# One matmul per tile for the state and the outputs of a delta-rule scan, with GpSimd masking the state's keys and adding the state

## The chip, the cores and the metric

The kernel runs on one core of a Trainium2 chip. The metric is the device time of one execution in microseconds (us). Data is 32-bit float throughout. The core has five engines that run side by side and meet at semaphores: TensorE (PE; its weight loads are listed apart as PEld), VectorE (DVE), ScalarE (ACT), GpSimd (POOL) and SyncE (SP), which here issues the DMAs.

## The reference, cut to what matters

A gated delta-rule layer, then layer norm, then a linear layer with a low-rank addition, then layer norm. The input is 32 sequences of 512 tokens of width 256, 8 heads of 32. The costly part is the recurrence over the tokens: each (sequence, head) has a 32x32 state `S` that is read with the key, corrected, read with the query and decayed:

```
q, k, v = silu(x @ Wq), silu(x @ Wk), silu(x @ Wv);  k = k / |k|
beta = 2 * sigmoid(x @ Wbeta);  log_f = log_sigmoid(x @ Wf1 @ Wf2)
for every token, in two half steps (decay with the first, k v^T and the output with the second):
    bS = b_t . S
    S  = exp(g) * S + a_t (x) bS + k_t (x) v_t          # a_t = -beta * k (* exp(log_f)), b_t = k
    o  = q_t . S
y = rms_norm_per_head(o * sigmoid(x @ Wog1 @ Wog2)) * norm_w @ Wo
x = layernorm(x + y);  x = layernorm(x + x @ W^T + b + x @ lilora^T)
```

## The kernel before

The tokens are cut into blocks of 8 (`TB`), a block's 16 half steps (`ROWS`) are solved at once with the inverse of a 16x16 triangular matrix, and the blocks of a sequence follow each other through the state. Two sequences share a tile of 32 rows (`GB` = 2), four heads fill the 128 partitions (four quarters of 32), and a second half of four heads is a second tile, so a **chunk** is 8 tiles (`CT`) of 128x32. 512 tokens make a **group** of 8 chunks (`CH`); there are 32 groups (`G`).

PE works in **slots**, one a chunk, 8 a group (`slot`, L738). Slot n does three pieces of 32x32 work, each piece on the four quarters of the array side by side:

- `deltas` (L720): the inverse `t_now` times the right sides `x_now` of chunk n-1, into `p2_bank`;
- `updates` (L708), for chunk n-2: for each tile and head one matmul with the keys `w_now` stationary and `parts` moving (64 columns: the deltas of the one sequence, then of the other, the rest zero), which is the change of the state (`ds_bank`), and one with `delta` stationary and the masked query weights `aq_now` moving (16 columns), which is the part of the outputs that comes from within the block (`o_bank`);
- `right_sides` (L728): the state `s_now` with the keys and queries `uq_now` of chunk n, into `p1_bank` (24 columns).

Behind these three each slot has its own piece of dense work for other groups (`dense0` to `dense7`): slots 0 and 1 hold projections and four `scores` (L700, 48 columns), slot 2 the key projection and `turn_scores`, slot 3 the query projection and more, slot 4 `feed_forward`, slot 5 `sums`, slot 6 the output projection, slot 7 the transposes of the inverse. Every engine runs its own list in its written order, with semaphore waits in between; there is no scheduler.

Around a slot, once `updates` has finished (semaphore `p3_filled`): ACT copies `p2_bank` three times (`delta_part`, L851: masked for each of the two sequences into `parts`, plain into `delta`). DVE (`update`, L1073) subtracts the output parts (L1087, twice) and adds `ds_bank` to the state into `moved` (L1093); POOL multiplies `moved` with the decay back into `state` (`decay_part`, L473). When `right_sides` has finished, DVE subtracts the values (L1100) and turns the block (L1103) into `x_now`; ACT copies the queries' part (`query_part`, L863). SP stages the next operands (L382, L392, L394, L360, L361). Between these steps of the scan DVE does the rest of its list in a fixed order: in slot 3 the first eight steps of the 16x16 inverse (`solve`, L1141 and L1145), in slot 4 the other seven, in slot 5 the feed-forward's addition, the cumulative sums (L1227), L1233 and L1239, in slot 6 L1246, L1250 and L1257, in slot 7 L1266 and, as its last, the decayed keys and queries of the next group but one (L1277, L1282). The last of these releases SP's `stage_uq` (L350), whose DMA `scores` waits for in slot 0.

## Time and profile before

| | |
|---|---|
| time, median of 3 runs | 2630.47 us (2616.48 to 2632.16) |
| span of the profiled execution, first to last instruction | 2622.0 us |
| median less that span | 8.5 us |
| PE busy | 2288.4 us (87%) |
| DVE busy | 1601.7 us (61%) |
| ACT busy | 1618.0 us (62%) |
| POOL busy | 458.8 us (17%) |
| PE's share of the chain that ended last | 86%, and 10% issue |

The time of the profiled execution itself is not among the numbers shown; its span is, and the median stands 8.5 us above it. A share is a mean over the span: the stretches differ, and in a group of some 76 us DVE is far busier in slots 4 to 7 than in slots 0 to 3. "Issue" in the chain is time in which PE waits for nothing that the profile shows. The first window of rows 5 below holds slots 4 to 7 of a group, the second its slots 0 to 3. A matmul of 32-bit floats is two records on PE, so that the 32 matmuls of 64 columns in a slot are 64 records.

### The profile page before, as it was taken

How to read it: one execution, taken by the hardware profiler on the slowest of the kernel's cores; microseconds unless marked ns; L12 is line 12 of the kernel's file. 1: busy time of each engine (PE TensorE's matmuls, PEld its weight loads, DVE VectorE, ACT ScalarE, POOL GpSimd, SP SyncE). 2: the span in 40 equal slices, each digit the busy share in tenths (PEclk: the TensorE clock that was granted, in tenths of full speed). 3: DMA queues.
4: the chain of work that ended last, by engine and by line, in shares of the span. 5: the costliest groups of instructions: out<-in, count | busy, mean ns of one | idle time of the engine just before them, and what ended most of it. 6: DMA issues, size and time to landing. Idle time of an engine off the chain costs nothing.

```text
span 2622.0 us, 225147 instructions
## 1 busy us (share of the span) xinstructions
PE 2288.4 (87%) x102472; PEld 1721.9 (66%) x102472; DVE 1601.7 (61%) x3940; ACT 1618.0 (62%) x3048; POOL 458.8 (17%) x555
## 2 busy tenths in 40 slices
PE   6788898999988899998999998989999988999785
PEld 2556666666666666666676666666666666766573
DVE  2456366666556676656666665666666566666533
ACT  3556466666666666656666666666666666666543
POOL 1011111111111111111111111111111111111210
PEclk7879899999999999999999999999999999999987
DMA  3244455534555554455554455555445555534541
GB/s 95 74 110 121 110 148 148 141 104 127 145 141 151 137 141 111 132 138 146 144 137 118 124 145 146 148 141 142 113 129 143 145 148 148 136 103 132 140 125 41
DMA packets 692934, 338.90 MB, mean 129 GB/s; under 512 B 551794, under 2 KB 651728, under 8 KB 692816
## 3 DMA queue, kind: packets, MB, share of 16 engines
q1 hardware_dynamic: 692816, 337.67, 48.2%
q14 instruction: 86, 0.70, 0.1%
q8 instruction: 32, 0.52, 0.1%
HBM read 35.57 MB, written 16.78 MB: 20 GB/s over the span
## 4 chain that ended last, share of the span: by engine, by line
PE 86%; issue 10%; DVE 2%; ACT 1%; DMA 1%; SPq 0%; ACTq 0%; DVEq 0%
PE bank L570 14%; PE bank L733 13%; PE bank L712 11%; PE bank L704 8%; PE bank L724 7%; PE bank L716 5%; PE bank L593 5%; PE bank L683 5%; PE bank L622 5%; PE bank L643 3%; PE bank L577 3%; PE bank L694 2%; PE bank L602 2%; PE bank L587 2%; PE bank L584 2%
## 5 line engine op out<-in xcount | busy, mean ns | idle before, releaser
L473 POOL TENSOR_TENSOR state<-moved,edge 128x512 f32<-128x512 f32 x252 | 292.3, 1160 | 1821.9 <-DVE moved L1093 1821.9
L712 PE MATMUL bank<-parts,w_now 32*32 32x64 f32 x16512 | 420.1, 223 | 4.8 <-DMA w_now<-w_row 3.6
L570 PE MATMUL bank<-x_col,w_kqv 128*128 128x512 f32 x768 | 370.6, 619 | 48.5 <-issue 47.9
L856 ACT ACTIVATE parts<-bank,cf 128x256 f32<-128x256 f32 x512 | 214.6, 470 | 319.5 <-DVE o_col L1087 310.7
L716 PE MATMUL bank<-aq_now,delta 32*32 32x16 f32 x16512 | 403.7, 179 | 9.2 <-issue 9.2
L716 PEld LDWEIGHTS bank<-aq_now,delta 32*32 32x32 f32 x16512 | 391.7, 110 | 6.7 <-issue 6.7
L712 PEld LDWEIGHTS bank<-parts,w_now 32*32 32x32 f32 x16512 | 377.2, 110 | 17.1 <-issue 5.0
L733 PE MATMUL bank<-uq_now,s_now 32*32 32x24 f32 x32768 | 362.2, 189 | 14.5 <-issue 14.4
L733 PEld LDWEIGHTS bank<-uq_now,s_now 32*32 32x32 f32 x32768 | 337.1, 107 | 24.1 <-issue 18.2
L1116 DVE COPY_PREDICATED aq<-ci,bank 128x128 f32<-128x128 int32 x256 | 77.1, 301 | 410.3 <-PE bank L704 276.7
L1087 DVE TENSOR_TENSOR o_col<-qs,bank 128x64 f32<-128x64 f32 x512 | 89.5, 216 | 388.6 <-PE bank L716 384.7
L724 PEld LDWEIGHTS bank<-x_now,t_now 32*32 32x32 f32 x16448 | 172.7, 107 | 149.6 <-issue 147.7
L570 PEld LDWEIGHTS bank<-x_col,w_kqv 128*128 128x128 f32 x768 | 138.5, 193 | 189.7 <-issue 184.8
L724 PE MATMUL bank<-x_now,t_now 32*32 32x32 f32 x16448 | 199.6, 196 | 61.5 <-issue 50.6
L900 ACT ACTIVATE a_low<-bank 128x256 f32<-128x256 f32 x256 | 133.9, 625 | 153.0 <-PE bank L704 153.0
L863 ACT ACTIVATE qs<-bank 128x128 f32<-128x128 f32 x256 | 71.3, 278 | 195.2 <-DVE x_now L1103 194.5
L1145 DVE TENSOR_TENSOR inv<-inv,prod 128x60 f32<-128x60 f32 (+7 forms) x480 | 169.4, 353 | 16.5
L1141 DVE TENSOR_TENSOR prod<-low,inv 128x60 f32<-128x60 f32 (+7 forms) x480 | 165.9, 346 | 17.4 <-ACT low L971 4.1
L1093 DVE TENSOR_TENSOR moved<-state,bank 128x512 f32<-128x512 f32 x256 | 173.9, 679 | 0.0
L704 PEld LDWEIGHTS bank<-uq_a,w_a 32*32 32x32 f32 x8192 | 109.2, 116 | 85.9 <-issue 71.5
L704 PE MATMUL bank<-uq_a,w_a 32*32 32x48 f32 x8192 | 117.9, 217 | 30.7 <-issue 17.9
L683 PE MATMUL bank<-w_out,y_col 128*128 128x256 f32 x512 | 119.8, 388 | 27.3 <-issue 23.9
(99 smaller groups left out, 3814.1 us busy)
## 6 DMA issues: line engine op xcount, KB each, us to landing
s_now<-state SPq DMA_DIRECT2D x256, 256.0 KB
uq_now<-uqv SPq DMA_DIRECT2D x256, 192.0 KB
t_now<-t_t SPq DMA_DIRECT2D x256, 128.0 KB, 2.0
w_now<-w_row SPq DMA_DIRECT2D x256, 128.0 KB
uq_a<-uqv SPq DMA_DIRECT2D x64, 384.0 KB
low<-uqv SPq DMA_DIRECT2D x64, 384.0 KB
x_col<-in_xt_dram SPq DMA_DIRECT2D x32, 512.0 KB, 5.8
w_a<-w_col SPq DMA_DIRECT2D x64, 256.0 KB
```

The costliest lines, as they stand in the source:

```text
L473: pool.tensor_tensor(state[:, qc, :, :, :].rearrange("p m b v -> p (m b) v"), moved[m % 2][:, :, :, :].rearrange("p m b v -> p (m b) v"), ...
L570: mm = pe.matmul(ps[:, :], w_kqv[:, a, w, f * P:(f + 1) * P], x_col[:, a, :], start=a == 0, stop=a == KT - 1)
L683: mm = pe.matmul(ps[:, t * D:(t + 1) * D], y_col[:, f, own], w_out[:, f, :], start=f == 0, stop=f == HF - 1)
L704: mm = pe.matmul(a_banks[m // CT][quarter(h), m % CT, :, :].rearrange("p b r -> p (b r)"), w_a[c][quarter(h), m, :], uq_of(uq_a[c], m % HF ...
L712: pe.matmul(ds_bank[quarter(h), m, :, :].rearrange("p b v -> p (b v)"), w_now[quarter(h), m, :], parts[quarter(h), m, :, :].rearrange("p b ...
L716: mm = pe.matmul(o_bank[quarter(h), m, :], delta[quarter(h), m, :], aq_now[quarter(h), m, :], start=True, stop=True)
L724: mm = pe.matmul(p2_bank[quarter(h), m, :], t_now[quarter(h), m, :], x_now[quarter(h), m, :], start=True, stop=True)
L733: mm = pe.matmul(p1_bank[quarter(h), m, b, :], s_now[quarter(h), m, b, :], uq_of(uq_now, m % HF)[quarter(h), m // HF, b * RQ:(b + 1) * RQ] ...
L856: act.activation(parts[:, :, b, :], p2_bank, ACT.Copy, scale=cf[:, C_TAKE + b:C_TAKE + b + 1])
L1093: dve.tensor_tensor(moved[m % 2][:, :, :, :], mine, ds_bank, ALU.add).then_inc(s_added.handle, 1)
L1141: dve.tensor_tensor(step, low[:, p + 1:ROWS, :, p:p + 1].to_broadcast(size), inv[:, p:p + 1, :, 0:width].to_broadcast(size), ALU.mult).the ...
L1145: dve.tensor_tensor(inv[:, p + 1:ROWS, :, 0:width], inv[:, p + 1:ROWS, :, 0:width], step, ALU.add).then_inc(solve_step.handle, 1)
```

## The change

- The masked deltas `parts` are gone. Instead the keys are masked: POOL writes `w_row` twice, once for each sequence, into a new operand `wa_now` (`mask_part`, two instructions a slot of 128x256), which lies beside the query weights; the query weights come by DMA as before, the DMA of `w_now` is gone.
- `updates` is one matmul for each tile and head: `delta` stationary, the 80 columns of `wa_now` moving, in five pieces of 16 contiguous columns. The change of the state comes out turned.
- So DVE, instead of adding, turns the change back with two transposes of 128x256 into `change`, and POOL adds `change` to `state` (new, 128x512) and then decays it (as before).
- `delta_part` on ACT is one instruction in place of three. It waits for DVE's transposes too, since deltas and updates now lie in the same two banks.
- PE's waits are fewer: `deltas` waits for the staging and for `qs_copied` (before: `x_turned`, `delta_ready`, `o_added` and the staging), `updates` for `w_masked`.

```diff
+    PIECE = GB * TB
+    WIDE = GB * HD + PIECE
+    PIECES = WIDE // PIECE
...
-        w_now = sb("w_now", [P, CT, HD])
-        parts = sb("parts", [P, CT, GB, HD])
-        aq_now = sb("aq_now", [P, CT, GB * TB])
+        wa_now = sb("wa_now", [P, PIECES, CT, PIECE])
...
-        moved = [sb(f"moved{c}", [P, CT, GB, HD]) for c in range(2)]
+        change = [sb(f"change{c}", [P, CT, GB, HD]) for c in range(2)]
...
-        psum = [ctx.enter_context(nc.psum_tensor(f"bank{i}", [P, BANK], F32)) for i in range(8)]
+        wide = ctx.enter_context(nc.psum_tensor("wide", [P, HF, BANK], F32))
+        single = [ctx.enter_context(nc.psum_tensor(f"bank{i}", [P, BANK], F32)) for i in range(6)]
+        psum = [single[0], wide[:, 0, :], wide[:, 1, :]] + single[1:]
         p1_bank = psum[0][:, 0:CT * GB * RQ].rearrange("p (m b r) -> p m b r", m=CT, b=GB)
-        p2_bank = psum[1][:, 0:CT * HD].rearrange("p (m v) -> p m v", m=CT)
-        o_bank = psum[1][:, CT * HD:CT * (HD + GB * TB)].rearrange("p (m r) -> p m r", m=CT)
-        ds_bank = psum[2][:, :].rearrange("p (m b v) -> p m b v", m=CT, b=GB)
+        up_bank = wide[:, :, 0:QI * WIDE].rearrange("p f (q c) -> p f q c", c=WIDE)
+        p2_bank = wide[:, :, QI * WIDE:QI * (WIDE + HD)].rearrange("p f (q v) -> p f q v", v=HD)
...
-        uq_in = signal("uq_in", 16 * CH)
-        s_in = signal("s_in", 16 * CH)
-        t_in = signal("t_in", 16 * CH, primed=16)
-        aq_in = signal("aq_in", 16 * CH, primed=32)
-        w_in = signal("w_in", 16 * CH, primed=32)
+        first_in = signal("first_in", 32 * CH)
+        second_in = signal("second_in", 32 * CH, primed=48)
+        w_masked = signal("w_masked", GB * CH, primed=2 * GB)
...
-                        turned = held(sp, third, w_turned.at(g, 1))
                         if m == 0:
                             sp.wait_ge(aq_masked.handle, masked)
-                            sp.wait_ge(w_turned.handle, turned)
                         sp.wait_ge(p3_filled.handle, left)
-                        sp.dma_start(aq_now[:, :, :],
-                                     chunk(aq[c if n >= 1 else 1 - c], m)).then_inc(aq_in.handle, 16)
-                        sp.dma_start(by_pairs(w_now[:, :, :]),
-                                     of_chunks(by_pairs(w_row[c if n >= 1 else 1 - c][:, :, :]),
-                                               m)).then_inc(w_in.handle, 16)
+                        sp.dma_start(wa_now[:, PIECES - 1, :, :],
+                                     chunk(aq[c if n >= 1 else 1 - c], m)).then_inc(second_in.handle, 16)
...
+            def mask_part(j, c, n):
+
+                if not (there(j) and not (isinstance(j, int) and j * CH + n == 0) or (there(j - 1) and n < 1)):
+                    return
+                g, m, own = (j, n - 1, c) if n >= 1 else (j - 1, CH - 1, 1 - c)
+                rows = of_chunks(by_pairs(w_row[own][:, :, :]), m).rearrange("p q (f k e) -> p q f k e", f=HF, e=PIECE)
+                if m == 0:
+                    pool.wait_ge(w_turned.handle, w_turned.at(g, 1))
+                made = held(pool, until, p3_filled.at(j, n + 1))
+                pool.wait_ge(set_up.handle, N_SET_UP)
+                pool.wait_ge(p3_filled.handle, made)
+                for b in range(GB):
+                    dst = wa_now[:, 2 * b:2 * b + 2, :, :].rearrange("p k (q f) e -> p q f k e", f=HF)
+                    pool.tensor_scalar(dst, rows, cf[:, C_TAKE + b:C_TAKE + b + 1], None,
+                                       ALU.mult).then_inc(w_masked.handle, 1)
...
+                mine = state[:, qc, :, :, :].rearrange("p m b v -> p (m b) v")
+                pool.wait_ge(s_turned.handle, s_turned.at(g, m + 1))
+                pool.tensor_tensor(mine, mine, change[m % 2][:, :, :, :].rearrange("p m b v -> p (m b) v"),
+                                   ALU.add).then_inc(s_added.handle, 1)
                 pool.wait_ge(s_added.handle, s_added.at(g, m + 1))
                 decay = edge[own][:, blk, qc * QI:(qc + 1) * QI, :, :].rearrange("p q f b -> p (q f b)")
-                pool.tensor_tensor(state[:, qc, :, :, :].rearrange("p m b v -> p (m b) v"),
-                                   moved[m % 2][:, :, :, :].rearrange("p m b v -> p (m b) v"),
-                                   decay.unsqueeze(2).to_broadcast([P, CT * GB, HD]),
+                pool.tensor_tensor(mine, mine, decay.unsqueeze(2).to_broadcast([P, CT * GB, HD]),
                                    ALU.mult).then_inc(state_ready.handle, 1)
...
                 for n in range(4):
+                    mask_part(j, c, n)
...
                 for m in range(CT):
                     for h in range(HPH):
-                        pe.matmul(ds_bank[quarter(h), m, :, :].rearrange("p b v -> p (b v)"), w_now[quarter(h), m, :],
-                                  parts[quarter(h), m, :, :].rearrange("p b v -> p (b v)"),
-                                  start=True, stop=True)
-                    for h in range(HPH):
-                        mm = pe.matmul(o_bank[quarter(h), m, :], delta[quarter(h), m, :], aq_now[quarter(h), m, :],
-                                       start=True, stop=True)
+                        mm = pe.matmul(up_bank[quarter(h), m % HF, m // HF, :].rearrange("p (k e) -> p k e", e=PIECE),
+                                       delta[quarter(h), m, :], wa_now[quarter(h), :, m, :], start=True, stop=True)
                 mm.then_inc(p3_filled.handle, 1)
...
-                pe.wait_ge(x_turned.handle, turn)
-                pe.wait_ge(t_in.handle, turn16)
-                pe.wait_ge(delta_ready.handle, turn)
-                pe.wait_ge(o_added.handle, turn)
+                pe.wait_ge(second_in.handle, turn32)
+                pe.wait_ge(qs_copied.handle, turn)
                 deltas()
 
                 pe.wait_ge(set_up.handle, N_SET_UP)
-                pe.wait_ge(w_in.handle, turn16)
-                pe.wait_ge(aq_in.handle, turn16)
-                pe.wait_ge(s_added.handle, turn)
+                pe.wait_ge(w_masked.handle, turn2)
                 updates()
 
                 pe.wait_ge(set_up.handle, N_SET_UP)
-                pe.wait_ge(uq_in.handle, turn16)
-                pe.wait_ge(s_in.handle, turn16)
-                pe.wait_ge(qs_copied.handle, turn)
+                pe.wait_ge(first_in.handle, turn32)
                 right_sides()
...
-                act.wait_ge(o_added.handle, o_added.at(j, n - 1))
-                for b in range(GB):
-                    act.activation(parts[:, :, b, :], p2_bank, ACT.Copy, scale=cf[:, C_TAKE + b:C_TAKE + b + 1])
-                act.activation(delta[:, :, :], p2_bank, ACT.Copy).then_inc(delta_ready.handle, 1)
+                act.wait_ge(s_turned.handle, s_turned.at(j, n - 1))
+                act.activation(delta[:, :, :].rearrange("p (q f) v -> p f q v", f=HF), p2_bank,
+                               ACT.Copy).then_inc(delta_ready.handle, 1)
...
-                    src = o_bank.rearrange("p (q f) (b t) -> p q f b t", f=HF, b=GB)[:, :, f, :, :]
+                    src = up_bank[:, f, :, GB * HD:WIDE].rearrange("p q (b t) -> p q b t", b=GB)
                     more = qs[m % 4][:, :, :, :].rearrange("p (q f) b t -> p q f b t", f=HF)[:, :, f, :, :]
                     last = dve.tensor_tensor(dst, more, src, ALU.subtract)
                 last.then_inc(o_added.handle, 1)
                 if isinstance(g, int) and g == G - 1 and m > QC + 1:
-                    dve.wait_ge(s_added.handle, s_added.at(g, m - 1))
+                    pass
                 else:
                     dve.wait_ge(state_ready.handle, state_ready.at(g, m - 1))
-                dve.tensor_tensor(moved[m % 2][:, :, :, :], mine, ds_bank, ALU.add).then_inc(s_added.handle, 1)
+                dst = change[m % 2][:, :, :, :].rearrange("p (q f) b v -> p f q (b v)", f=HF)
+                for f in range(HF):
+                    last = dve.transpose(dst[:, f, :, :], up_bank[:, f, :, 0:GB * HD])
+                last.then_inc(s_turned.handle, 1)
```

The rows that follow are instructions in the order in which they stand on an engine, with no time in them. First GpSimd in the loop, from the bias additions (L487 before, L502 now) between slots 3 and 4 to the first scan work of slot 4. Before:

```order
L486 ISA [waits solve_step]
L487 TENSOR_TENSOR h_row<-h_row,bias_row 128x256 [waits ht_filled]
L487 TENSOR_TENSOR h_row<-h_row,bias_row 128x256
L486 REGISTER_ALU
L487 TENSOR_TENSOR h_row<-h_row,bias_row 128x256 [waits ht_filled]
L487 TENSOR_TENSOR h_row<-h_row,bias_row 128x256
L471 REGISTER_ALU
L473 TENSOR_TENSOR state<-moved,edge 128x512 [waits s_added]
```

And now:

```order
L501 ISA [waits solve_step]
L502 TENSOR_TENSOR h_row<-h_row,bias_row 128x256 [waits ht_filled]
L502 TENSOR_TENSOR h_row<-h_row,bias_row 128x256
L501 REGISTER_ALU
L502 TENSOR_TENSOR h_row<-h_row,bias_row 128x256 [waits ht_filled]
L502 TENSOR_TENSOR h_row<-h_row,bias_row 128x256
L280 ISA
L467 TENSOR_SCALAR wa_now<-w_row,cf 128x8x2x16 [waits p3_filled,set_up]
L467 TENSOR_SCALAR wa_now<-w_row,cf 128x8x2x16
L484 REGISTER_ALU
L485 TENSOR_TENSOR state<-state,change 128x512 [waits s_turned]
L489 TENSOR_TENSOR state<-state,edge 128x512 [waits s_added]
```

Where one decay stood there are now two masks, an addition and the decay, and the masks of slot 4 stand behind the bias additions, which wait for `solve_step` of DVE. Second VectorE in the loop, slot 6, from the output parts to L1250 (now L1259). Before:

```order
L1087 TENSOR_TENSOR o_col<-qs,bank 128x4x2x8 [waits qs_copied,p3_filled]
L1087 TENSOR_TENSOR o_col<-qs,bank 128x4x2x8
L1093 TENSOR_TENSOR moved<-state,bank 128x512 [waits state_ready]
L1100 TENSOR_TENSOR bank<-bank,uqv 128x16x8 [waits p1_filled]
L1103 STREAM_TRANSPOSE x_now<-bank 128x256 [waits p2_filled,v_taken]
L1246 TENSOR_TENSOR k_col<-k_col,ss_col 128x1024 [waits r_ready]
L1250 SCALAR_TENSOR_TENSOR kb_col<-kb_col,k_col 128x1024 [waits k_normed,beta_drained]
```

And now:

```order
L1093 TENSOR_TENSOR o_col<-qs,wide 128x4x2x8 [waits qs_copied,p3_filled]
L1093 TENSOR_TENSOR o_col<-qs,wide 128x4x2x8
L1101 STREAM_TRANSPOSE change<-wide 128x4x64 [waits state_ready]
L1101 STREAM_TRANSPOSE change<-wide 128x4x64
L1109 TENSOR_TENSOR bank<-bank,uqv 128x16x8 [waits p1_filled]
L1112 STREAM_TRANSPOSE x_now<-bank 128x256 [waits p2_filled,v_taken]
L1255 TENSOR_TENSOR k_col<-k_col,ss_col 128x1024 [waits r_ready]
L1259 SCALAR_TENSOR_TENSOR kb_col<-kb_col,k_col 128x1024 [waits k_normed,beta_drained]
```

The addition with one operand in SBUF and one in PSUM has become two transposes out of PSUM; the two-operand instructions behind `x_now` stand where they stood.

## Rows read from the trace of the kernel before

**Rows 1.** The page: span, PE's and DVE's line, and the chain's shares by engine.
```profile
span 2622.0 us, 225147 instructions
PE 2288.4 (87%) x102472; PEld 1721.9 (66%) x102472; DVE 1601.7 (61%) x3940; ACT 1618.0 (62%) x3048; POOL 458.8 (17%) x555
...
PE 86%; issue 10%; DVE 2%; ACT 1%; DMA 1%; SPq 0%; ACTq 0%; DVEq 0%
```
**Rows 2.** The chain in order of time, slot 5: start us, us, what.
```profile
1333.80 0.68 PE bank L724 x50
1334.48 0.25 PE bank L712 x6
...
1336.03 1.33 PE bank L733 x82
1337.36 0.67 issue
```
**Rows 3.** The timeline, weight loads of one projection: start us, us, engine, line, idle before.
```profile
1308.44 0.19 PEld L570 LDWEIGHTS bank<-x_col,w_kqv 128*128 128x128 f32 x1 [0.24 <-issue]
1308.87 0.19 PEld L570 LDWEIGHTS bank<-x_col,w_kqv 128*128 128x128 f32 x1 [0.24 <-issue]
```
**Rows 4.** The chain, slot 0: the issue gap ahead of the first scores.
```profile
1437.64 0.66 issue
1438.30 1.56 PE bank L704 x127
```
**Rows 5.** By window: us, busy PE, PEld, DVE, ACT, POOL; clock, DMA share, GB/s.
```profile
1403.80:1434.40 30.60, 27.55 (x1384) 23.09 (x1377) 28.35 (x58) 19.81 (x32) 6.21 (x9) 1.00 0.42 113
1359.00:1403.80 44.80, 40.53 (x1819) 28.32 (x1811) 21.26 (x64) 29.89 (x63) 7.87 (x8) 1.00 0.58 156
```
**Rows 6.** The timeline of DVE in slots 5, 6 and 7.
```profile
1411.71 0.35 DVE L1087 TENSOR_TENSOR o_col<-qs,bank 128x64 f32<-128x64 f32 x2 [0.23 <-PE bank L716]
...
1413.06 0.30 DVE L1100 TENSOR_TENSOR bank<-bank,uqv 128x128 f32<-128x128 f32 x1 [0.40 <-PE bank L733]
...
1420.52 0.68 DVE L1093 TENSOR_TENSOR moved<-state,bank 128x512 f32<-128x512 f32 x1
1421.12 0.29 DVE L1100 TENSOR_TENSOR bank<-bank,uqv 128x128 f32<-128x128 f32 x1
1421.44 0.45 DVE L1103 STREAM_TRANSPOSE x_now<-bank 128x256 f32<-128x256 f32 x1
1421.81 1.59 DVE L1246 TENSOR_TENSOR k_col<-k_col,ss_col 128x1024 f32<-128x1024 f32 x1
...
1427.68 0.35 DVE L1087 TENSOR_TENSOR o_col<-qs,bank 128x64 f32<-128x64 f32 x2 [0.54 <-PE bank L716]
...
1433.08 1.28 DVE L1282 TENSOR_TENSOR uqv<-q_col,ep 128x512 f32<-128x512 f32 x2
```
**Rows 7.** The timeline of SP: the staging that DVE's L1282 releases.
```profile
1434.43 0.59 SPq L350 DMA_DIRECT2D uq_a<-uqv  x1
```
**Rows 8.** The timeline of DVE and POOL, slot 1, then POOL in slot 6.
```profile
1371.66 1.22 DVE L1179 SCALAR_TENSOR_TENSOR y_col<-gate,o_col 128x1024 f32<-128x1024 f32 x1
...
1371.82 1.96 POOL L473 TENSOR_TENSOR state<-moved,edge 128x512 f32<-128x512 f32 x1 [11.06 <-DVE moved L1093]
...
1421.27 1.05 POOL L473 TENSOR_TENSOR state<-moved,edge 128x512 f32<-128x512 f32 x1 [7.49 <-DVE moved L1093]
```
**Rows 9.** The timeline: one solve step alone, and the same beside POOL.
```profile
1331.51 0.41 DVE L1145 TENSOR_TENSOR inv<-inv,prod 128x240 f32<-128x240 f32 x1
...
2481.44 1.14 DVE L1145 TENSOR_TENSOR inv<-inv,prod 128x240 f32<-128x240 f32 x1
...
2481.11 1.21 POOL L473 TENSOR_TENSOR state<-moved,edge 128x512 f32<-128x512 f32 x1
```
**Rows 10.** Groups by line: count, busy us, mean ns of one, idle before.
```profile
L473 POOL TENSOR_TENSOR state<-moved,edge 128x512 f32<-128x512 f32 x252 | 292.3, 1160 | 1821.9 <-DVE moved L1093 1821.9
L487 POOL TENSOR_TENSOR h_row<-h_row,bias_row 128x256 f32<-128x256 f32 x128 | 89.0, 726 | 240.7 <-DVE inv L1145 182.8 <-PE bank L612 57.9
L452 POOL MEMSET x_now<- 128x256 f32 x1 | 0.3, 315 | 0.0
```

43 lines of the change are left out of this document (23 added, 20 removed).

## The prediction, made before the result was known

> **What bounds the kernel now.** The page says PE: 86% of the chain and 10% issue [rows 1]. A mean over a span hides that a group of some 76 us has two halves, so I read the busy time by window next. In slots 0 to 3 DVE is busy 21.26 of 44.80 us; in slots 4 to 7 it is busy 28.35 of 30.60 us, more than PE with 27.55 [rows 5]. The timeline of DVE there shows the little that is left: it waits 0.23 us for PE at slot 5's update, 0.40 us for `right_sides` in slot 5, and 0.54 us at slot 7's update [rows 6]. At the end of that run of work stands L1282 (1433.08 + 1.28 = 1434.36), SP issues `uq_a` at 1434.43 [rows 7], and PE, which has come to its first `scores` at 1437.64, starts them at 1438.30 [rows 4], 3.94 us behind DVE's end. So a group has two bounds in turn: from the first scores of slot 0 to the update of slot 4 it is PE, and from there to the next first scores DVE and PE are level within about a microsecond, with DVE and then a DMA closing the stretch. A gain on PE counts in full in the first part; in the second only as far as DVE has idle time, and each microsecond that DVE gets longer beyond it is paid in full.
>
> **The change part by part, for one group.**
>
> *PE, `updates`.* It takes 1336.03 - 1334.48 = 1.55 us a slot [rows 2]: 128 records at 12 ns, no matter that half of them have 64 columns and half 16. After, it is 64 records of 80 columns. What a column costs: a record of 512 columns is 0.43 us [rows 3], so 0.84 ns a column. What a record costs beside its columns: `scores` has 128 records of 48 columns in 1.56 us [rows 4], so each quarter has 32 records of 40 ns (1.29 us), and 8.4 ns are left for each. Of 80 columns a quarter has 16 records of 67 + 8.4 ns: 1.21 us, and 0.34 us a slot is saved. Bounds: the columns alone, 1.07 us (0.48 saved), and nothing saved, if a moving operand in five pieces of 16 columns streams slower, of which no row shows a case. I take 0.34, since `scores` is the nearest row in kind. In slots 1 to 4 that is 4 x 0.34 = **1.36 us saved**; slots 5, 6, 7 and 0 lie beside DVE's stretch.
>
> The Trainium skill speaks against this step: "TensorE: Matmul & The Clock Gate", section "Wait — 56ns, not 53.3ns?", says that the start-to-start of matmuls never drops below about 25 ns. By it 64 records would take 1.6 us and the step would save nothing. The records here start every 12 ns over four quarters, so I let the row decide.
>
> *ACT.* Two of three copies of the deltas go. ACT is not what PE waits for in these stretches, so I cost it at nothing; its cover is that DVE's chain ends later. It now waits for the transposes, which is inside the 4 us that PE spends on `right_sides` and dense work.
>
> *SP.* A DMA of 128 KB a slot goes. The uq_a transfer is released by DVE alone: nothing gained.
>
> *DVE, own work.* The addition L1093 takes 1421.12 - 1420.52 = 0.60 us of DVE's time. A transpose of 128x256 out of PSUM takes 1421.81 - 1421.44 = 0.37 [rows 6], two take 0.74. So +0.14 a slot, in slots 5 to 7: **+0.42 us**. In slot 4 it vanishes in the wait for `right_sides`.
>
> *POOL, and what it does to DVE.* POOL had one instruction of 1.05 us a slot [rows 8]; it gets two masks and an addition more. POOL itself has room: 6.21 of 30.60 us busy [rows 5]. But look at rows 8. POOL's decay starts at 1371.82 while DVE runs a two-operand instruction out of SBUF until 1372.88; it takes 1.96 instead of 1.05, so it stood still for 0.91 of the 1.06 us of overlap. Rows 9 show the other side: the solve step that takes 0.41 alone takes 1.14 when POOL is in a decay, whose end is 0.88 after the step's start: 0.73 lost. In slot 6 L1246 takes 1.59, where a same-sized instruction takes 1.22 [rows 6, 8], beside POOL's decay at 1421.27 [rows 8]. So a two-operand DVE instruction and a POOL instruction exclude each other, first come, first served, and the later one loses the overlap less 0.15 us. The instructions behind `x_now` on DVE are such ones in slots 4 (solve), 6 (L1246) and 7 (L1277); the copies and transposes out of PSUM (L1087, L1100, L1103) are not slowed.
>
> The prices. Mask, 128x256, one operand: between 0.315 us (a memset of that size) and 0.726 us (L487, two operands) [rows 10]; I take the middle, 0.5. Addition, 128x512, two full operands: between 1.05 (the decay, whose second operand is broadcast) and 1.45 (twice L487) [rows 8, 10]; I take 1.2. The two now follow the transposes one after the other, so POOL is busy until 2.3 us behind them, where before it was done 1.05 us behind the addition; DVE's next instruction behind `x_now` starts 0.7 us behind them when DVE is late (1421.81 - 1421.12).
>
> - Slot 4: L1141 and L1145 meet the end of the addition (0.2) and the decay (0.8): 1.0 us.
> - Slot 5: DVE is now late, so the masks, which start when `updates` ends, meet the last solve steps (0.45); L1218 reads PSUM and is free; L1227 meets the decay's end (0.35): 0.8 us.
> - Slot 6: masks against L1233 and L1239, 2 x 0.35; then L1246 and L1250 against addition and decay, 1.1; 0.4 of that is paid already: 1.4 us.
> - Slot 7: masks against L1257, 0.6; the edge work of POOL later against L1277, 0.3: 0.9 us.
>
> Together 4.1 us. DVE's stretch grows by 4.1 + 0.42 less the idle time 0.23 + 0.40 + 0.54 = 1.17 that it can use up: **+3.35 us**. With -1.36 a group is 2.0 us longer. Thirty groups have the whole of this work (those for which a group after next exists): +60 us. I lay it on the median: 2630.5 + 60 = **2690 us** (the profiled span, 2622.0, would be 2682).
>
> On the masks the Trainium skill says more than the rows do: "SBUF — State Buffer", section "Who interferes with whom", has GpSimd share one pair of ports with DVE and any GpSimd instruction that reads SBUF stand against a two-operand one of DVE. The rows show it for two-operand POOL instructions only. By the page the masks count, as I have them; without them the loss is 1.75 us smaller and the group is 0.25 us longer, no measurable change.
>
> **The rivals.**
>
> 1. *Faster: the exclusion is seldom met.* If POOL's instructions find the gaps, or DVE's two-operand work waits less than in rows 9, DVE has only its own +0.14. Then slot 5's lateness drowns in its 0.40 wait and the stretch shortens by 0.34 (slot 5) and by 0.54 - 0.28 = 0.26 (slot 7's idle time less two updates); with 1.36 that is 1.96 us a group, 59 in all: 2571 us. For it: in slots 4 of the trace a solve step is 0.41 us as a rule [rows 9]. Against it: that is because the decay ends before the solve starts, and with a second POOL instruction of 1.2 us ahead of it it cannot. The point that decides is the loss in slots 4 to 7: below about 2 us a group the change wins.
> 2. *The two cancel.* Half the loss, 2.1 us, or masks that DVE does not feel: 0 a group, 2630 us, and 2604 to 2657 counts as the same.
> 3. *`updates` gets no shorter* (the strided pieces, or a floor for each matmul): +3.35 us a group, 2731 us. For it: no matmul here reads its moving operand in pieces. Against it: 0.84 ns a column is slow beside what one contiguous run needs.
> 4. *POOL itself becomes the bound.* Its work in slot 6 and 7 is 3.25 us of 8, stretched by exclusion; `s_now` has a whole slot of slack. It would need more than twice that: I leave it in the tail.
>
> **How the numbers follow.** Less or more than 1% (26 us) is what a measurement here can tell from no change. Forecast 0.47, rival 1 0.25, rival 2 0.20, rival 3 and worse 0.08. Faster 0.25, same 0.20, slower 0.55. The unknown prices move a group by -0.95 to +1.1 (five masks), -0.45 to +0.75 (three additions), -0.56 to +1.36 (PE): the forecast's own range is 2640 to 2765, with all three at their worst 2786. The range of 8 in 10 reaches down to rival 1, 2570, and up to 2765.
>
> **What the changed profile would show.** `updates` from its first record to the first of `right_sides`: 1.21 us at the full clock. Of the solve steps in slot 4, one or two at 0.9 to 1.3 us instead of 0.4, in every group. L1246 (its new line) at 1.6 or more and L1250 longer than 1.23. DVE without idle time from slot 5 to slot 0. POOL's mask at 0.5 and addition at 1.2, some of them near 2. The issue gap ahead of the first scores in slot 0 grows from 0.66 to about 2 us, and gaps ahead of the dense work of slot 6 or of `deltas` in slots 7 and 0, since `y_col` and `x_now` come late. I am wrong if the solve steps keep their 0.4 us, or if DVE still waits for PE in slots 5 to 7.

## The result

The changed kernel takes 2679.5 us (median of 4 runs, 2653.2 to 2687.0), the kernel before 2631.3 us (4 runs): a ratio of 1.019, interval 1.012 to 1.025. It is slower by 48 us, by 1.2 to 2.5%, which is clear of no change. Forecast were 2690 us and +60 us, by a gain on PE that a loss on DVE outweighs. The profiled execution took 2680.97 us with a span of 2679.2 us.

The page of the kernel after, in the same order as [rows 1] and [rows 10]: span, PE's and DVE's line, the chain's shares by engine, and then POOL's groups (count, busy us, mean ns of one, idle before).

```profile
span 2679.2 us, 192080 instructions
PE 2224.3 (83%) x85960; PEld 1650.9 (62%) x85960; DVE 1828.6 (68%) x4196; ACT 1436.3 (54%) x2536; POOL 1356.7 (51%) x1317
...
PE 58%; DVE 25%; issue 15%; ACT 1%; DMA 1%; DVEq 0%; SPq 0%; ACTq 0%
...
L467 POOL TENSOR_SCALAR wa_now<-w_row,cf 128x256 f32<-128x256 f32 x512 | 519.6, 1025 | 919.9 <-PE wide L729 918.6
...
L485 POOL TENSOR_TENSOR state<-state,change 128x512 f32<-128x512 f32 x252 | 349.4, 1386 | 80.9 <-DVE change L1101 80.9
...
L489 POOL TENSOR_TENSOR state<-state,edge 128x512 f32<-128x512 f32 x252 | 294.2, 1167 | 19.8
```

PE has 64 us less to do and POOL 898 us more, and DVE, whose own work hardly grew, is busy for 227 us more. DVE's share of the chain goes from 2% to 25%. Two windows of one group answer to [rows 5], first the part that closes with DVE, then the part that PE bounds. The second begins at the first scores, where that of [rows 5] began 3.5 us ahead of them (1362.46), so its 39.50 us compare with 41.3 and not with 44.80:

```profile
1343.70:1378.40 34.70, 27.81 (x1206) 22.56 (x1194) 33.76 (x63) 17.64 (x25) 24.67 (x25) 1.00 0.32 91
1304.20:1343.70 39.50, 36.23 (x1495) 25.53 (x1496) 20.52 (x55) 25.99 (x53) 14.07 (x15) 1.00 0.53 146
```

I cut every group of both traces at the same three marks: **A** from the first scores of slot 0 to the end of slot 4's updates, **B** from there to the end of DVE's last instruction for the staging of `uq_a`, **C** from there to the next first scores. The means, worked out from the start and end times in the traces, in us (before 27 groups, after 28; "clock A" is the mean granted clock in A; DVE idle is in B):

```
                        A      B      C    group   DVE idle  clock A
before                42.80  30.71  3.78   77.28     2.35     0.963
after                 41.29  34.81  3.91   80.01     1.29     0.952
```

The 28th group of before is left out because its C is 12.5 us instead of 3.8, with PE stopped for 2.8 us inside its updates and for 3.9 inside its right sides.

The longer B holds the loss. Where it sits on DVE, by instruction, in us a group of B, before and after: the solve steps (L1141 and L1145, now L1150 and L1154) 4.59 and 6.73; the scan (L1227, L1236) 2.61 and 3.19; `y_col` (L1239, L1248) 1.33 and 1.72; `k_col` and `kb_col` (L1246 and L1250, L1255 and L1259) 2.74 and 3.58; `w_col` 2.41 and 2.70; `uqv` (L1277 and L1282, L1286 and L1291) 3.83 and 4.64. That is 5.05 us more in instructions whose own work the edit didn't touch. The edited instructions themselves cost 0.12 more: the transposes 2.76 for an addition of 2.39, and 0.25 less in copies and subtractions beside them. 1.06 us came out of idle time. Together 4.1 us.

Slot 4 of the same group shows how it happens. POOL's timeline (start us, us, what), then DVE's:

```profile
1342.82 2.77 POOL L502 TENSOR_TENSOR h_row<-h_row,bias_row 128x256 f32<-128x256 f32 x4 [5.97 <-DVE inv L1154]
1345.57 2.00 POOL L467 TENSOR_SCALAR wa_now<-w_row,cf 128x256 f32<-128x256 f32 x2
1347.54 1.41 POOL L485 TENSOR_TENSOR state<-state,change 128x512 f32<-128x512 f32 x1
1349.02 1.07 POOL L489 TENSOR_TENSOR state<-state,edge 128x512 f32<-128x512 f32 x1
```

```profile
1344.01 0.77 DVE L1101 STREAM_TRANSPOSE change<-wide 128x256 f32<-128x256 f32 x2
...
1347.41 0.41 DVE L1154 TENSOR_TENSOR inv<-inv,prod 128x240 f32<-128x240 f32 x1
1347.85 1.33 DVE L1150 TENSOR_TENSOR prod<-low,inv 128x220 f32<-128x220 f32 x1
1349.22 1.12 DVE L1154 TENSOR_TENSOR inv<-inv,prod 128x220 f32<-128x220 f32 x1
```

The transposes are done at 1344.78, but POOL has four additions of the bias and two masks in its queue first and comes to the addition at 1347.54. Addition and decay then lie on two solve steps that take 0.39 us alone; they take 1.33 and 1.12. Each ends 0.23 to 0.25 us behind POOL's instruction.

The end of the group on the chain of waits, to be read beside [rows 2, 4]:

```profile
1373.35 0.46 DVE x_now L1112
1373.83 0.29 ACT qs L870
1374.12 0.14 issue
1374.26 0.77 PE wide L737 x51
1375.02 1.14 PE wide L729 x62
1376.16 1.12 PE bank L746 x79
1377.28 0.41 issue
1377.70 1.98 PE bank L587 x4
1379.68 2.61 issue
1382.28 1.56 PE bank L721 x127
```

`updates` is down from 1.55 to 1.14 us, and PE stands for 2.61 us ahead of the first scores where it stood for 0.66. The `deltas` of slot 0 (L737) wait for DVE's `x_now` and ACT's `qs`.

### The profile page after: what moved, and what is told of

It is laid out like the page before. It is cut to its first block, busy times and chain, and to the rows that moved or that the text cites. A ratio compares the mean times of both kernels' runs of the same rounds, so it can differ in the third digit from the quotient of the medians.

```text
span 2679.2 us, 192080 instructions
## 1 busy us (share of the span) xinstructions
PE 2224.3 (83%) x85960; PEld 1650.9 (62%) x85960; DVE 1828.6 (68%) x4196; ACT 1436.3 (54%) x2536; POOL 1356.7 (51%) x1317
## 4 chain that ended last, share of the span: by engine, by line
PE 58%; DVE 25%; issue 15%; ACT 1%; DMA 1%; DVEq 0%; SPq 0%; ACTq 0%
PE bank L587 14%; PE wide L729 8%; PE bank L721 8%; PE bank L746 8%; PE wide L737 5%; DVE prod L1150 4%; DVE inv L1154 4%; DVE dd L1236 3%; PE bank L660 3%; DVE w_col L1266 3%; DVE change L1101 2%; PE bank L594 2%; PE bank L619 2%; PE bank L604 2%; DVE k_col L1255 2%
## 5 line engine op out<-in xcount | busy, mean ns | idle before, releaser
L467 POOL TENSOR_SCALAR wa_now<-w_row,cf 128x256 f32<-128x256 f32 x512 | 519.6, 1025 | 919.9 <-PE wide L729 918.6
L485 POOL TENSOR_TENSOR state<-state,change 128x512 f32<-128x512 f32 x252 | 349.4, 1386 | 80.9 <-DVE change L1101 80.9
L729 PE MATMUL wide<-wa_now,delta 32*32 32x80 f32 x16512 | 376.3, 244 | 4.6 <-POOL wa_now L467 4.6
L863 ACT ACTIVATE delta<-wide 128x256 f32<-128x256 f32 x256 | 98.4, 384 | 522.9 <-DVE change L1101 521.1
L729 PEld LDWEIGHTS wide<-wa_now,delta 32*32 32x32 f32 x16512 | 332.0, 114 | 4.9 <-issue 2.5
L489 POOL TENSOR_TENSOR state<-state,edge 128x512 f32<-128x512 f32 x252 | 294.2, 1167 | 19.8
L1093 DVE TENSOR_TENSOR o_col<-qs,wide 128x64 f32<-128x64 f32 x512 | 88.8, 214 | 281.6 <-PE wide L729 278.0
L737 PEld LDWEIGHTS wide<-x_now,t_now 32*32 32x32 f32 x16448 | 181.0, 110 | 154.9 <-issue 154.1
L737 PE MATMUL wide<-x_now,t_now 32*32 32x32 f32 x16448 | 208.5, 199 | 60.0 <-issue 40.6
L1154 DVE TENSOR_TENSOR inv<-inv,prod 128x60 f32<-128x60 f32 (+7 forms) x480 | 233.7, 487 | 16.5
L1150 DVE TENSOR_TENSOR prod<-low,inv 128x60 f32<-128x60 f32 (+7 forms) x480 | 224.5, 468 | 17.4 <-ACT low L978 4.1
L1101 DVE STREAM_TRANSPOSE change<-wide 128x256 f32<-128x256 f32 x512 | 197.3, 422 | 1.3
L502 POOL TENSOR_TENSOR h_row<-h_row,bias_row 128x256 f32<-128x256 f32 x128 | 88.8, 726 | 202.3 <-DVE inv L1154 167.4
```

Of the source, the lines that this page charges most:

```text
L467: pool.tensor_scalar(dst, rows, cf[:, C_TAKE + b:C_TAKE + b + 1], None, ALU.mult).then_inc(w_masked.handle, 1)
L485: pool.tensor_tensor(mine, mine, change[m % 2][:, :, :, :].rearrange("p m b v -> p (m b) v"), ALU.add).then_inc(s_added.handle, 1)
L489: pool.tensor_tensor(mine, mine, decay.unsqueeze(2).to_broadcast([P, CT * GB, HD]), ALU.mult).then_inc(state_ready.handle, 1)
L729: mm = pe.matmul(up_bank[quarter(h), m % HF, m // HF, :].rearrange("p (k e) -> p k e", e=PIECE), delta[quarter(h), m, :], wa_now[quarter(h ...
L737: mm = pe.matmul(p2_bank[quarter(h), m % HF, m // HF, :], t_now[quarter(h), m, :], x_now[quarter(h), m, :], start=True, stop=True)
L1101: last = dve.transpose(dst[:, f, :, :], up_bank[:, f, :, 0:GB * HD])
```

## The experiments

Eleven kernels ran. The time is a median; where a kernel ran more than once, the ratio is to the kernel before on the same chip. A single run gives no interval, and for those kernels the argument rests on A and B. These are means over 28 groups, for before_early over 27. The kernel before took 2618.9 us beside the first four, 2622.5 beside the next four and 2620.8 beside masks_behind, before_early and act_masks_early_bias.

```
                        us     ratio (interval)         A      B    group  DVE idle
act_masks             2632.7  1.005 (1.003 to 1.007)  41.79  32.73  78.47    1.09
tiny_masks            2649.9  one run                 42.01  32.88  78.87    1.08
no_add                2551.9  one run                 40.60  30.97  75.49    1.08
no_both               2555.5  0.976 (0.973 to 0.979)  41.75  29.81  75.82    1.12
act_masks_pool_read   2674.4  one run                 41.45  34.49  79.84    1.27
act_masks_pool_write  2660.4  one run                 41.48  33.78  79.25    1.10
act_masks_dve_add     2653.6  1.010 (1.006 to 1.015)  42.15  32.75  78.89    1.20
act_masks_early       2604.7  0.993 (0.990 to 0.996)  41.35  32.08  77.39    0.91
masks_behind          2672.4  1.017 (1.010 to 1.025)  41.58  34.42  79.95    1.07
before_early          2624.6  1.002 (0.998 to 1.005)  42.68  30.79  77.22    4.07
act_masks_early_bias  2600.7  0.992 (0.988 to 0.995)  42.08  31.88  77.91    1.20
```

### The masks and the addition, one at a time

**Masks on ACT.** Theory: POOL's two new kinds of work lengthen DVE's. Rival: the loss is elsewhere (DVE's own transposes, the later `x_now`).

```
 def delta_part(j, c, n):                                   # ACT
     act.wait_ge(p3_filled.handle, p3_filled.at(j, n + 1))
+    for b in range(GB):
+        act.activation(dst, rows, ACT.Copy, scale=cf[:, C_TAKE + b:C_TAKE + b + 1])
-    pool.tensor_scalar(dst, rows, cf[:, C_TAKE + b:C_TAKE + b + 1], None, ALU.mult)
```

> The whole computation; the two masks stand on ACT ahead of its copy of the deltas instead of on POOL. Theory (exclusion between POOL's instructions and DVE's two-operand ones): DVE's stretch from slot 4's update to its L1291 shrinks from 34.8 us to about 32.5, since POOL's 1.84 us of masks a slot no longer meet DVE; PE's stretch stays at 41.3; about 2615 us, level with or a little under the kernel before. Rival A (the stretch is longer because deltas now waits for qs_copied and ACT for the transposes): ACT has even more ahead of its copy, the stretch stays at 34.8 or grows, 2680 us or more. Rival B (the lower clock after slot 3): no change either, 2680 us.

B is 2.08 us shorter than after, 32.73. The solve steps fall from 6.73 to 5.54 us a group, `y_col` is back at 1.33 and `w_col` at 2.41, while the scan stays at 3.19. The time is 2632.7, not the 2615 expected, and A is half a microsecond longer, with its mean clock at 0.933.

**Masks of eight elements a partition, still on POOL** (W is masked in those elements alone).

```
-    rows = ...rearrange("p q (f k e) -> p q f k e", ...)
+    rows = ...rearrange("p q (f k e) -> p q f k e", ...)[:, 0:1, 0, :, 0:1]
```

> Left out: nearly all of the masking. Each of POOL's two mask instructions a slot handles 8 elements a partition instead of 256 and most of wa_now stays zero; waits and order are as in the changed kernel. Exclusion: DVE's stretch 34.8 -> about 32.3 us, 2610 us. Rival A (new waits): all waits are there, so 34.8 stays. The masks' cost alone, without any more work on ACT.

B is 32.88, the same as with the masks on ACT (32.3 expected), and the time 2649.9 (2610 expected), with A at 42.01. Each small mask still takes 0.29 us. So the gain of B doesn't come from the engine that masks, but from POOL having less to do.

**No addition** (the state's running sum is left out; the decay reads `change`), and **neither**.

```
-    pool.tensor_tensor(mine, mine, change[m % 2], ALU.add)
-    pool.tensor_tensor(mine, mine, decay, ALU.mult)
+    pool.tensor_tensor(mine, change[m % 2], decay, ALU.mult)
```

> Left out: the addition of the change to the state; POOL decays the change itself, behind the same wait for the transposes. Exclusion: POOL is busy 1.27 us less behind the transposes, DVE's stretch 34.8 -> about 33.3 us, some 2635 us. Rival A: 34.8 stays, since every wait of DVE, ACT and PE is as it was.

> Left out: both the masking (nearly) and the addition to the state. POOL has about its old work, while PE, DVE and ACT have the changed one. Exclusion: DVE's stretch falls to about 30.2 us, under the 30.7 of before, PE's stays 41.3, and the time is my rival of a change without exclusion, 2570 us. Rival A (new waits): the stretch stays near 34 and the time above 2650. Rival B (clock): the stretch falls, but the PE stretch keeps a granted clock near 0.95 and gives less than 1.6 us over the kernel before.

I had this wrong by far for no_add: 83 us too much. B falls by 3.84 us, where I had expected 1.5. The two by two of B reads: both 34.81, addition alone 32.88, masks alone 30.97, neither 29.81. The addition costs 3.1 us without the masks and 3.8 with them; the masks cost 1.2 alone and 1.9 with it. The surplus of 0.8 us is what they do to each other. Without both, DVE's groups of instructions (by shape) are back at the kernel before's, where they took 1568, 745 and 1226 ns:

```profile
L1252 DVE TENSOR_TENSOR k_col<-k_col,ss_col 128x1024 f32<-128x1024 f32 x32 | 51.1, 1598 | 0.0
L1245 DVE SCALAR_TENSOR_TENSOR y_col<-y_col,norm_col,r_col 128x512 f32<-128x512 f32 x64 | 45.2, 748 | 8.4 <-ACT r_col L1023 8.4
L1256 DVE SCALAR_TENSOR_TENSOR kb_col<-kb_col,k_col 128x1024 f32<-128x1024 f32 x32 | 39.2, 1225 | 3.5
```

In the kernel after the same three are

```profile
L1259 DVE SCALAR_TENSOR_TENSOR kb_col<-kb_col,k_col 128x1024 f32<-128x1024 f32 x32 | 59.7, 1866 | 3.6
L1248 DVE SCALAR_TENSOR_TENSOR y_col<-y_col,norm_col,r_col 128x512 f32<-128x512 f32 x64 | 56.9, 929 | 9.0 <-ACT r_col L1026 9.0
L1255 DVE TENSOR_TENSOR k_col<-k_col,ss_col 128x1024 f32<-128x1024 f32 x32 | 55.0, 1720 | 0.0
```

`kb_col`, 1225 ns alone, meets the decay in nearly every group of the kernel after; `k_col` meets it in each kernel. And no_both is 2.4% faster than before, with the work left out: about that much the change's matmuls would be worth if POOL's new work cost nothing.

### Is it that POOL reads, or that it is busy?

Both kernels have the masks on ACT and idle POOL work in their old place, whose result goes to a scratch tile.

```
+    pool.tensor_scalar(idle, cf[:, 0:256] in pieces of 16, cf[:, C_TAKE + b:...], None, ALU.mult)   # x2, reads
+    pool.memset(idle[:, :], 0.0)                                                                    # x6, writes only
```

> The kernel after with the two masks on ACT, and in their old place on POOL two idle instructions of the masks' form (128x256, one operand from SBUF in pieces of 16, result to a scratch tile that nobody reads), released by the same wait. If what the masks cost is that POOL reads SBUF beside two-operand DVE work, the stretch from slot 4's update to DVE's last instruction goes back from 32.7 us (masks on ACT) to 34.8 us as in the kernel after, each idle instruction takes about 0.92 us alone and up to 2 us beside DVE, and the run comes out near 2680 us. Rival: the masks cost because PE's updates wait for POOL (the masks start late behind the decay); idle instructions hold nobody, so the stretch stays near 32.7 us and the time near 2635 us.

> The same with masks on ACT, but the idle POOL work is six memsets of 128x256, which read nothing: 6 x 0.315 = 1.9 us of POOL a slot, as much as the two masks. If only reading counts, the stretch stays near 32.7 us and the time near 2635 us, and each memset keeps 0.3 us beside two-operand DVE work. If any POOL access to SBUF excludes such DVE work, the stretch is 34 to 35 us and the time 2670 to 2690 us.

The reading form brings back 1.76 of the 2.08 us, so it isn't a wait for the masks: nobody waits for these. The memsets bring back 1.05, although the theory of reading gave them nothing. The groups of the two kernels, reading first and then writing, tell why, beside those of act_masks, which has neither:

```profile
L1237 DVE SCALAR_TENSOR_TENSOR y_col<-y_col,norm_col,r_col 128x512 f32<-128x512 f32 x64 | 45.0, 745 | 9.0 <-ACT r_col L1015 9.0
...
L1139 DVE TENSOR_TENSOR prod<-low,inv 128x240 f32<-128x240 f32 x64 | 27.1, 423 | 2.2
```

```profile
L1256 DVE SCALAR_TENSOR_TENSOR y_col<-y_col,norm_col,r_col 128x512 f32<-128x512 f32 x64 | 49.1, 806 | 9.0 <-ACT r_col L1034 9.0
...
L1158 DVE TENSOR_TENSOR prod<-low,inv 128x240 f32<-128x240 f32 x64 | 47.5, 742 | 2.2
...
L467 POOL TENSOR_SCALAR idle<-cf 128x256 f32<-128x256 f32 x512 | 530.0, 1035 | 975.2 <-PE wide L730 927.9 <-POOL idle L467 43.0 <-issue 3.7
```

```profile
L1254 DVE SCALAR_TENSOR_TENSOR y_col<-y_col,norm_col,r_col 128x512 f32<-128x512 f32 x64 | 45.1, 746 | 9.0 <-ACT r_col L1032 9.0
L1156 DVE TENSOR_TENSOR prod<-low,inv 128x240 f32<-128x240 f32 x64 | 38.8, 606 | 2.2
...
L467 POOL MEMSET idle<- 128x256 f32 x1536 | 478.8, 312 | 1054.9 <-PE wide L728 864.6 <-issue 32.0 <-POOL idle L467 11.8
```

The memsets keep their 312 ns and DVE's `y_col`, which lies beside them, its 746. Over all its two-operand instructions that overlap a memset alone, DVE loses nothing (0.276 us for 0.276, 0.409 for 0.409, 0.680 for 0.680). But the mean of the solve step goes from 423 ns in act_masks (409 alone) to 606 with the memsets too: not beside them, but beside the addition and the decay, which six memsets (2.5 us) have pushed back onto it. Slot 4 shows it; POOL's timeline, then DVE's, where the step of 220 elements takes 0.39 us beside a memset and 1.39 beside the addition:

```profile
1339.70 1.17 POOL L467 MEMSET idle<- 128x256 f32 x3
1340.83 1.26 POOL L484 TENSOR_TENSOR state<-state,change 128x512 f32<-128x512 f32 x1
```

```profile
1340.53 0.39 DVE L1156 TENSOR_TENSOR prod<-low,inv 128x220 f32<-128x220 f32 x1
1340.95 1.39 DVE L1160 TENSOR_TENSOR inv<-inv,prod 128x220 f32<-128x220 f32 x1
```

In slot 2 the decay ends 3.8 us behind the updates with the masks on ACT, 5.4 with the memsets, 4.6 with the masks on POOL (in slot 4, behind the bias, 3.9, 6.7 and 5.2). So the masks cost in two ways: what they read, and what they delay. How much is which stays open, since six memsets hold POOL for 2.5 us and two masks for 1.8.

The two-operand instruction out of SBUF is not the only kind that stands against POOL. In the kernel with memsets `dd<-dd`, one operand, 1024 elements at 0.67 ns each, often meets the delayed decay:

```profile
1342.18 1.07 POOL L488 TENSOR_TENSOR state<-state,edge 128x512 f32<-128x512 f32 x1
```

```profile
1342.27 1.53 DVE L1222 TENSOR_SCALAR dd<-dd 128x1024 f32<-128x1024 f32 x1
```

It takes 0.69 alone, which is faster for each element than the two-operand `kb_col` (1024 elements in 1.23). The Trainium skill ("SBUF — State Buffer", section "Who interferes with whom") has this: a DVE instruction with two inputs from SBUF stands against GpSimd work that reads SBUF and not against work that only writes; a one-input instruction does so when it runs in a two-port mode. The traces agree as far as they go, with 746 for 746 ns beside memsets, 806 for 746 beside reading, and 1.53 for 0.69; in which mode `dd<-dd` runs no trace shows.

### The masks behind the decay

```
 for n in range(4, CH):
+    if n < 6:                 # slots 4 and 5
+        decay_part(j, c, n)   # addition and decay
+        mask_part(j, c, n)
+        continue
     mask_part(j, c, n)
     decay_part(j, c, n)
```

> The whole computation of the kernel after, with one edit: in slots 4 and 5 POOL's queue has the addition and the decay first and the two masks behind them. Theory: the masks cost little by what they read (DVE's two-operand instructions lose about 0.05 to 0.2 us beside one); they cost because they keep POOL for 1.9 us, so that addition and decay end 5.0 us behind the updates instead of 3.8 us and lie on DVE's solve steps. Then the solve steps in the stretch from slot 4's update to DVE's last instruction fall from 6.7 us a group to 5.5 to 6.0, slot 5's update starts 1.3 to 1.6 us behind the matmuls instead of 2.4, the stretch is 33.4 to 34 us instead of 34.8 and the time 2640 to 2660 us. Rival: it is the masks' reading itself; then they cost the same on the later solve steps, the stretch stays at 34.5 to 35 us and the time at 2670 to 2690 us.

This went the rival's way: 2672.4 us, a ratio of 1.017 beside 1.019 for the kernel after. The solve steps do fall, from 6.73 to 6.09 us a group, but the scan rises from 3.19 to 3.68 and `y_col` from 1.72 to 1.78: the addition takes as long as before, and in slot 5 it now lies on the scan. Putting POOL's work in another order moved the collisions and took 0.4 us of B away, where taking the masks off POOL takes 2.1.

### The addition on DVE

```
     last.then_inc(s_turned.handle, 1)            # behind the transposes
+    dve.tensor_tensor(state[:, qc], state[:, qc], change[m % 2], ALU.add)
-    pool.tensor_tensor(mine, mine, change[m % 2], ALU.add)
```

> The whole computation with the masks on ACT and the addition of the change to the state on DVE, right behind its two transposes; POOL keeps the decay alone as in the kernel before. The addition of 128x512 from SBUF is estimated at 0.65 to 0.8 us of DVE (0.42 us for 252 elements, 0.60 us for 512 with one operand in PSUM), so DVE gets about 3 x 0.7 = 2.1 us more in slots 5 to 7. Without the addition on POOL the stretch was 3.1 us shorter (29.8 against 32.9 us with the masks out of the way). Theory of exclusion: 32.7 - 3.1 + 2.1 = 31.7 us, the first part as with masks on ACT, 77.5 us a group and about 2605 us. Rival: what the addition costs is DVE's and POOL's chain of state (transpose, addition, decay, stage) and not the exclusion; then moving it to DVE keeps the chain and adds 2.1 us, 34.8 us and 2690 us.

```profile
L1092 DVE TENSOR_TENSOR state<-state,change 128x512 f32<-128x512 f32 x256 | 177.6, 694 | 40.1 <-issue 14.6
```

The solve steps, the scan and `uqv` are back at 4.99, 2.61 and 3.83 us, so what the addition did to the scan and `uqv` is gone, and most of it on the solve steps (4.59 before); but B holds four such additions and not three, 2.77 us, and stays at 32.75. I had expected 31.7 and 2605 us; the time is 2653.6, with A at 42.15 us and its mean clock at 0.926. For B, 0.69 us paid on DVE is the same as 1.27 us on POOL that costs DVE about 0.8.

### Work moved out of the stretch

```
 turn_part(3)
-solve(j + 1, 0, 8)
+solve(j + 1, 0, 11)
 ...
 turn_part(4)
-solve(j + 1, 8, 11)
```

> The whole computation, masks on ACT, addition on POOL as in the change, and the last three solve steps of slot 4 (6 two-operand DVE instructions) moved into slot 3, where DVE has idle time. If slot 4's solve steps beside POOL's addition and decay are what lengthens that slot (8.8 us against 7.9 before, with three steps of 2 x 0.4 to 1.2 us), the stretch gets 2 to 3 us shorter, about 30.2 us, the group 76 to 76.5 and the time near 2560 to 2570 us. Rival: slot 4 is bound by PE's dense work and its clock; then DVE only waits longer in slot 5 and the time stays at 2620 to 2635 us.

> The kernel before with the same three solve steps moved from slot 4 into slot 3; it tells how much of the gain of moving them belongs to the change. In the kernel before DVE meets POOL rarely (solve steps 4.6 us in the stretch, 4.2 is their time alone) and DVE has 2.3 us of idle time there. Theory: about 2.3 us of DVE's work leave the stretch; slot 3 has 8 steps already and becomes bound by DVE, about 1 us late; net 0.5 to 1.5 us a group, 2580 to 2610 us. Rival: the stretch of the kernel before is bound by PE (27.6 of 30.6 us busy) as much as by DVE, and nothing is gained: 2620 to 2630 us.

> The whole computation, masks on ACT, three solve steps early, and POOL's four additions of the bias (3.4 us, up to now beside the last solve steps of slot 3) held back until those eleven steps are done. Theory: the five or six steps that took 0.8 instead of 0.42 us get back to 0.42, slot 4's update starts 0.3 us behind the matmuls instead of 1.5; in slot 4 the bias then keeps POOL, so addition and decay end 2 us later and meet the last four steps, which gives 0.5 to 1 us back: the group 0.5 to 1 us shorter than with the early steps alone, 2575 to 2595 us. Rival: POOL's order moves the loss only: addition and decay of slot 4 lose on the solve steps and the scan what slot 3 gains, 2600 to 2615 us.

act_masks_early computes everything and is 0.7% faster than the kernel before, 0.993 (0.990 to 0.996), and so faster than the kernel after, whose ratio is 1.019. Expected were 2560 to 2570 us, and it takes 2604.7. The gain of B is 0.65 us, not 2 to 3, since slot 3 becomes late instead. The timeline of DVE at the end of slot 3 says why; POOL's line first:

```profile
1380.12 3.44 POOL L485 TENSOR_TENSOR h_row<-h_row,bias_row 128x256 f32<-128x256 f32 x4 [5.96 <-DVE inv L1143]
```

```profile
1379.99 0.42 DVE L1139 TENSOR_TENSOR prod<-low,inv 128x252 f32<-128x252 f32 x1
1380.45 0.83 DVE L1143 TENSOR_TENSOR inv<-inv,prod 128x252 f32<-128x252 f32 x1
1381.31 0.82 DVE L1139 TENSOR_TENSOR prod<-low,inv 128x240 f32<-128x240 f32 x1
1382.16 0.82 DVE L1143 TENSOR_TENSOR inv<-inv,prod 128x240 f32<-128x240 f32 x1
```

The moved steps run under POOL's bias and take twice their time. Holding the bias back until they are done puts slot 4's update where it was (0.3 us behind the matmuls instead of 1.5), and a group whose A has the full clock takes 75.45 us instead of 75.94 (8 and 11 groups). But the clock is lower more often, the mean group is 77.91 against 77.39, and the time, 2600.7 us or 0.992 (0.988 to 0.995), is the same within the intervals, in the rival's range of 2600 to 2615.

The same edit to the kernel before does nothing, 1.002 (0.998 to 1.005). DVE's idle time in B goes from 2.35 to 4.07 us and B keeps its length, 30.79: there PE bounds B as much as DVE does. So B of the kernel before stands at a floor that is not DVE's, by its busy time PE's (27.55 of 30.60 us in [rows 5]), and with the shorter updates that floor is at most the 29.8 us of no_both.

Where the 26.5 us of act_masks_early against before lie (2595.5 and 2622.0 us of span): 18.5 ahead of the first full group, 4.1 in the 28 groups together, 3.9 behind them. The 4.1 are less than what the long last group of before adds (84.5 us, 7.2 above its mean): group by group act_masks_early is level with the kernel before.

## Why the prediction was right

**The balance and its sign: right.** A shrank and B grew by more. From the traces: A -1.51 us (forecast -1.36), B +4.10 (forecast +3.35), C +0.13, or +2.7 us a group (forecast +2.0), 76 us for 28 groups. The 28 groups from the first full one are 69.1 us longer, since the last of them takes 84.5 us before, 7.2 above the mean; ahead of them and behind them the change won 11.9 us, which I had put at nothing. Together the 57.2 us between the spans. That the forecast of 60 us came so close is luck in part: the loss of a group was put a quarter too small, and the gain outside the full groups at nothing.

**PE's updates: direction right, size too small.** 1.10 us a slot in the median (1.14 on the chain above), against 1.50 before. I had 1.21, with 1.07 as the bound of columns alone. `deltas` got shorter too, from 0.72 to 0.61 us in slots 3 and 5, which I had not foreseen. Over four slots the two make some 1.9 us. Where A runs at the full granted clock throughout, it takes 39.33 us after (7 groups) and 41.40 before (9 groups): 2.07 us less. Deciding by the row was right: 64 records in 1.10 us start every 17 ns over the four quarters. The floor of 25 ns that the Trainium skill gives ("TensorE: Matmul & The Clock Gate", section "Wait — 56ns, not 53.3ns?") does not bound matmuls that go to four quarters in turn, not even if the two records of a matmul are counted as one: the 32 matmuls of `deltas` take 0.61 us, one every 19 ns.

**The clock: missed.** I took no account of it. In slot 4 of 12 of 28 groups before, and of 21 after, the updates run at the lower level (2.1 us of 1.1). The mean clock in A goes from 0.963 to 0.952. Of the 2.07 us saved in A the mean keeps 1.51; the 0.56 between them go with the lower clock. act_masks has it in 23 slots 4 and in 15 slots 0, and its A is 2.5 us over the full-clock value of 39.30. What brings a group into this was not tried; it isn't POOL alone, since no_both has 19 such slots and no_add 13.

**DVE's own work: right.** +0.12 us a group, forecast +0.42; the eight transposes of B cost 0.35 each ([rows 6] gave 0.37) and the addition 0.60 as forecast, and the instructions beside them got 0.25 shorter.

**The exclusion: right in kind.** 5.05 us a group, forecast 4.1. By slots: the solve steps 2.14 (1.0 and 0.45 forecast), the scan 0.58 (0.35), `y_col` 0.39 and the instruction ahead of it none (0.7), `k_col` and `kb_col` 0.84 (0.7), `w_col` 0.29 (0.6), `uqv` 0.81 (0.3). Of the idle time 1.06 us was used up, forecast 1.17.

**The price of the mask: wrong, the step that failed.** I took 0.5 us, between 0.315 and 0.726; alone it takes 0.92 and in the mean 1.03, outside the bounds. Neither neighbour writes in pieces of 16. With 0.5 the two masks would be done before DVE's transposes are, and POOL would start the addition on time; with 0.92 they are not, and the bias stands ahead of them in slot 4 as well, which I did not look at. On the solve steps the masks cost 1.19 us (6.73 against 5.54 in act_masks) and not 0.45, and that is what the sum lacked there; the other 0.95 fit the 1.0 forecast. That the pieces of 16 are what makes the mask slow is not shown: no run had it without them. The addition was well priced, 1.27 alone for 1.2.

**Which of the two costs: half wrong.** I put 1.75 of the 4.1 us on the masks and so 2.35 on addition and decay. The runs say 1.2 to 1.9 for the masks and 3.1 to 3.8 for the addition alone. That the masks' share came out is luck: each lasts nearly twice as long as I had it, but takes less from DVE than I had it. A mask of 0.92 us costs `y_col` 0.22, where I had counted 0.35 for a mask of 0.5, and with the masks off POOL `y_col` and `w_col` together are 0.68 us shorter, where I had 1.3 with the instruction ahead of `y_col`.

**The rivals.** "Seldom met" is out: the loss is 5 us, not under 2. Its price was nearly right, though: no_both is 63 us faster, where that rival had 59. "The two cancel" is the case of act_masks. "No shorter updates" and "POOL the bound" are out.

**The marks foretold.** The solve steps at 0.9 to 1.3 us: 1.33 and 1.12. L1255 above 1.6: 1.72, and L1259 above 1.23: 1.87. DVE without idle time from slot 5 on: so. The gap ahead of the scores at about 2 us: 2.61. The mask at 0.5: no. My range has a slip: with all three prices at their best the sum is 2631 us, with all at their worst 2786, and neither end of 2640 to 2765 comes out of the terms named.

## What to carry to other kernels

Before you give work to GpSimd, list the VectorE instructions that will run beside it. Count each that reads two operands from SBUF as lost for as long as a two-operand GpSimd instruction lies on it; a one-operand one cost `y_col` a quarter of its own time here (0.22 of 0.92 us), and one that only writes cost nothing. The fast one-operand `dd<-dd` was held up too. Where VectorE closes a stretch, that is paid in full. Count also what already stands in GpSimd's queue and what the new work pushes back, since the pushed instruction may be the one that collides. And price a strided pattern by a strided row, or widen the bound beyond both contiguous neighbours.

## What the runs showed of the hardware

- A GpSimd instruction of 128x256 that reads one operand and writes pieces of 16 elements takes 0.92 us, against 0.73 us for two operands without pieces. ACT does two of the same masks in 0.91 us, half of POOL's time.
- One DVE instruction of 0.75 us that runs beside a mask for its whole length loses 0.22 us; beside an addition or a decay it loses nearly the whole overlap (0.39 becomes 1.33). The one-operand mask takes part of what the two-operand work takes.
- GpSimd writes alone (memsets, 312 ns each) neither slow DVE nor get slowed.
- The low granted clock, 1.2 GHz, comes in stretches shorter than a slot (in the kernel after, for one, from 627.3 to 630.7 us, over slot 4's updates) and costs a group 1.3 us for one such stretch in A and 2.6 for two (A of 39.3, 40.7 and 41.9 us in groups of act_masks_early, act_masks_pool_write and act_masks). It falls on some groups and not on others of one kernel; what brings it stays open.
- On four quarters in turn, 64 matmuls of 64 and 16 columns (128 records) take 1.50 us and 32 of 80 columns (64 records) 1.10; in the one the records start every 12 ns, in the other every 17 ns.
